# The order of ScalarE's side work in a Mamba scan: SiLUs at step 9, two normalizations at other steps

## The reference

```python
h = layernorm(layernorm(x)) * norm_w + norm_b
h = h @ in_proj_w.T                                   # 512 inner channels
h = silu(causal convolution of h, 4 taps, per channel)
dt_in, B, C = split(h @ x_proj_w.T, [1, 16, 16])
dt = softplus(dt_in @ dt_proj_w.T + dt_proj_b)
state[t] = exp(A * dt[t]) * state[t-1] + B[t] * h[t]  # 512 channels x 16 states
y[t] = sum over states (state[t] * C[t]) + D * h[t]
x1 = x + layernorm(silu(y) @ out_proj_w.T + layernorm(x))
```

## Time and profile before

| | us |
|---|---|
| median of 3 runs | 1411.33 (1410.96 to 1411.51) |
| the profiled execution, its own time | 1411.09 |
| its span in the profile | 1409.3 |
| mean granted TensorE clock | 0.941 of full speed |

### The profile page before, as it was taken

One profiled execution on the slowest core, in us unless ns is written; L12 is line 12 of the kernel. 1 busy time (PEld: TensorE's weight loads), 2 busy tenths in 40 slices (PEclk: granted clock), 3 DMA queues, 4 the chain that ended last, 5 costly groups with the idle time before them and its releaser, 6 DMA issues.

```text
span 1409.3 us, 15754 instructions
## 1 busy us (share of the span) xinstructions
PE 1175.4 (83%) x4782; PEld 518.5 (37%) x4783; DVE 1089.8 (77%) x1449; ACT 770.9 (55%) x1275; POOL 1088.4 (77%) x565
## 2 busy tenths in 40 slices
PE   5667678787886987888789688788999999999996
PEld 2222223222321422322233142233556655566653
DVE  3599999999999999999999989799241115776675
ACT  5757468676876866867686686556431111111111
POOL 0489999999999999999999999999122814444553
PEclk9898899999899999989998999999999999999998
DMA  3921211240150122014015012300269522222220
GB/s 108 274 68 62 90 60 32 75 150 0 65 192 1 62 91 106 32 75 149 1 66 175 1 62 90 134 0 31 90 238 324 162 71 82 81 81 79 83 67 15
DMA packets 72075, 127.71 MB, mean 91 GB/s; under 512 B 8759, under 2 KB 48448, under 8 KB 67904
## 3 DMA queue, kind: packets, MB, share of 16 engines
q1 hardware_dynamic: 60432, 103.72, 22.2%
q0 software_dynamic: 7152, 16.81, 3.7%
q10 hardware_dynamic: 4416, 6.29, 1.3%
HBM read 97.79 MB, written 31.76 MB: 92 GB/s over the span
## 4 chain that ended last, share of the span: by engine, by line
PE 36%; POOL 29%; issue 15%; DVE 12%; ACT 8%; DMA 0%; POOLq 0%; ACTq 0%; SPq 0%; DVEq 0%
POOL state L511 18%; PE psX L1647 10%; POOL bx L500 9%; DVE state L1090 6%; PE psX L1582 5%; PE psY L1595 3%; PE psY L1664 2%; PE bank L1664 2%; PE psY L1529 2%; PE bank L1451 2%; POOL lt L516 2%; ACT psX L763 2%; PE bank L1486 1%; DVE bx L1078 1%; DVE acc L1025 1%
## 5 line engine op out<-in xcount | busy, mean ns | idle before, releaser
L511 POOL TENSOR_TENSOR state<-state,cbc 128x1024 f32<-128x1024 f32 x256 | 606.6, 2398 | 14.9 <-DVE state L1090 14.8
L1090 DVE TENSOR_TENSOR_SCAN state<-psX,bx 128x1024 f32<-128x1024 f32 x256 | 578.5, 2279 | 38.5 <-ACT psX L763 23.1
L763 ACT ACTIVATE psX<-dt,aneg 128x511 f32<-128x511 f32 x512 | 330.7, 679 | 199.0 <-DVE state L1090 197.6
L500 POOL TENSOR_TENSOR bx<-xh,bbc 128x1024 f32<-128x1024 f32 x120 | 291.1, 2426 | 59.5 <-DMA bbc<-bc_rows 43.1
L1529 PE MATMUL psY<-state,ident 64*64 64x512 f32 x2048 | 287.5, 654 | 20.3 <-POOL state L511 20.0
L1486 PE MATMUL bank<-prow,ident 128*128 128x512 f32 x272 | 169.9, 710 | 113.3 <-DVE bx L1078 113.3
L1078 DVE TENSOR_TENSOR bx<-xh,bank 128x1024 f32<-128x1024 f32 x136 | 162.7, 1196 | 7.7 <-PE bank L1486 7.6
L1529 PEld LDWEIGHTS psY<-state,ident 64*64 64x64 f32 x2048 | 63.9, 140 | 206.8 <-issue 126.2
L961 ACT ACTIVATE sg<-psX 128x512 f32<-128x512 f32 x39 | 23.3, 597 | 196.5 <-PE psX L1647 196.5
L1486 PEld LDWEIGHTS bank<-prow,ident 128*128 128x128 f32 x272 | 48.0, 209 | 206.9 <-DVE bx L1078 166.9
L581 POOL DMA_INDIRECT ysl<-shared_rows,idx x39 | 40.3, 1033 | 80.6 <-DVE idx L1258 75.9
(11 more groups left out here) (200 smaller groups left out, 1718.8 us busy)
## 6 DMA issues: line engine op xcount, KB each, us to landing
cbc<-bc_rows SPq DMA_DIRECT2D x32, 1024.0 KB, 5.0
bbc<-bc_rows SPq DMA_DIRECT2D x16, 1024.0 KB, 6.2
slot_in<-ao SPq DMA_DIRECT2D x1, 5011.5 KB, 35.1
xsl<-slot_in SPq DMA_DIRECT2D x39, 128.5 KB, 2.0
xin<-in_x SPq DMA_DIRECT2D x8, 512.0 KB, 4.5
xr<-in_x SPq DMA_DIRECT2D x8, 512.0 KB, 5.5
x_rows<-ao SPq DMA_DIRECT2D x8, 512.0 KB, 2.9
xn_rows<-xr SPq DMA_DIRECT2D x8, 512.0 KB, 3.2
```

Of the source, the lines that this page charges most:

```text
L500: nc.gpsimd.tensor_tensor(bx[q % RB][:], xh[par][:, h * CH:(h + 1) * CH], bbc[:, n // 2].unsqueeze(1).broadcast_to([P, CH, L]), ALU.mult). ...
L511: nc.gpsimd.tensor_tensor(w[:], w[:], cbc[:, n].unsqueeze(1).broadcast_to([P, CH, L]), ALU.mult).then_inc(weighted, 1)
L763: e = nc.scalar.activation(decay[q % RD][:, c, 1:L], dt[par][:, h * CH + c, 1:L], ACT.Exp, scale=aneg[:, h * CH + c, n:n + 1])
L1090: nc.vector.tensor_tensor_scan(st[q % RS][:].rearrange("p c t -> p (c t)"), decay[q % RD].rearrange("p c t -> p (c t)"), bx[q % RB][:].rea ...
```

## The change

All three edits are on ACT's stream and in its loop over the steps. (1) The SiLU for xh, the SiLU of y and that of the shared expert, with the load of their table set before and of the other set behind, are issued at step 9 and not at step 10: after the decays for scan 11, ahead of those for scan 12. (2) The moments of `lead` (the input of batch i + 2) are computed at step 24 and not at step 29; their `apply` stays at steps 30 and 31. (3) At steps 26 and 27 `back` comes ahead of `front`: `moments(2)` and the normalizing of xn stand ahead of the second and third copy of dt. The calls behind the loop follow the new step number; the order of the work there is as before. No instruction is added or removed.

```diff
             def lead(f, par, q):
-                if q == 29:
+                if q == 24:
                     act.wait_ge(mv0_ready, f + 1)
                     moments(3, f, mv0[par], 1.0 + EPS, eps2c)
...
             def front(f, par, q):
...
-                if q == 10:
+                if q == 9:
                     act.wait_ge(conv_done, C * (f + 1))
                     if not (isinstance(f, int) and f < 2):
                         act.wait_ge(y_kept, H * (f - 1))
                     nc.scalar.activation(xh[par][:], acc[:], ACT.Silu).then_inc(xh_ready, 1)
...
             def back(b, q):
...
-                if q == 10:
+                if q == 9:
                     act.wait_ge(y_kept, H * (b + 1))
                     nc.scalar.activation(yv[:], yv[:], ACT.Silu).then_inc(ys_ready, 1)
...
             def early(q):
...
-                if q == 10:
+                if q == 9:
                     act.wait_ge(e_gate_kept, FC)
                     nc.scalar.activation(acc[:], acc[:], ACT.Silu).then_inc(e_silu, 1)
...
             def iteration(i, par, do_lead, do_front, do_scan, do_back):
...
+                    if do_back and q in (26, 27):
+                        back(i - 1, q)
                     if do_front:
                         front(i + 1, 1 - par, q)
-                    if do_back:
+                    if do_back and q not in (26, 27):
                         back(i - 1, q)
                     if not do_front:
                         early(q)
-                    if q == 10 and (do_front or do_back):
+                    if q == 9 and (do_front or do_back):
                         ln_exp_tables()
...
-            for q in range(10):
+            for q in range(9):
                 back(NB - 1, q)
             keep_y(NB - 1, 1)
-            back(NB - 1, 10)
+            back(NB - 1, 9)
```

## The result

The changed kernel takes 1413.97 us (median of 20 runs, 1412.78 to 1416.42); the kernel before, run beside it, 1411.53 us (20 runs, 1410.09 to 1414.35). The ratio is 1.0017, 95% interval 1.0011 to 1.0023: about 2.4 us slower, where the forecast was 9 us faster and the range ended at 1410.5. Of every program one execution was profiled; the changed kernel's took 1414.7 us, with a span of 1412.9.

A forecast was written before the change was run, and what follows sets the result against it. POOL's own work and a slightly longer chain over all engines bound the scan iterations, POOL's waits capping the gain. Terms of 0.65 + 1.7 + 2 x 1.15 + 2 x 2.1 = 8.85 us gave 1402.4 us, range 1398 to 1410.5.

The forecast's parts named there:

- The bound: In the scan iterations, POOL's work and a chain over all engines run almost level; POOL's waits cap the gain.
- The sum up to iteration 6: Gains of 0.65 us from iteration 0, 1.7 from 1, 1.15 per short and 2.1 per long interval: 8.85 us.
- The lead moments: Moved from step 29 to 24, they free scan 0's decays: 1.46 us won in long intervals, 1.25 in short.
- long interval: The intervals after iterations 3 and 5, with POOL waits of about 3 us; short ones follow 2 and 4.
- The swap: Moments and normalizing ahead of dt's copies, steps 26 and 27: 0.4 us won in long intervals, 0.3 lost in short.
- the sign of being wrong: Steps 26 and 27: second dt copy over 1 us late in all iterations, with PE behind it.
- The SiLUs, 0.2 us: SiLUs and table loads from step 10 to 9: chain gains 0.2 us per iteration, bounds 0 and 0.7.
- so it doesn't: Step 9, iteration 4: the table load need not wait for the convolution; scan 12 has 0.5 us in hand.
- After iteration 6 there is nothing to win: Behind iteration 6 POOL has no more waits, so no gain was counted there.
- The sentence on the tail's SiLU: The tail's SiLU moves by one step number only and keeps its place; no size given.
- Its start follows line 516 by a fixed distance, which the change leaves alone: Argument against the slower case: the start of DVE's minimum at steps 22 and 23 keeps its distance.
- The rival: Slower: DVE's minimum is held up against POOL, 5 us per event, a loss from the third on; chance 0.10.

The follow-up runs named there:

- a_again: The changed kernel unaltered, in a second set of runs: 1414.06 us, ratio 1.0015 to the kernel before.
- d_mom: The kernel before with only the lead moments moved from step 29 to 24: 1405.78 us, ratio 0.9963.
- d_swap: The kernel before with only the order at steps 26 and 27 changed: 1414.18 us, ratio 1.0016.
- a_silu7: The changed kernel with the SiLUs and table loads of iteration 7 alone back at step 10: 1410.65 us, ratio 0.9993.
- d_silu: The kernel before with only the SiLUs and their table loads moved to step 9: 1418.17 us, ratio 1.0033.
- d_mom_swap: The kernel before with the moments at step 24 and the new order at steps 26 and 27, SiLUs left at step 10: 1404.38 us, ratio 0.9951.
- a7_delay: a_silu7 plus four useless DVE statistics (1.4 us) at step 18 of iteration 6 only, delaying scan 19: 1404.47 us, ratio 0.995.

## Why the prediction was wrong, step by step

**The bound: right.** POOL against a chain over all engines, with POOL's waits at step 19 as the cap. The cap was even reached: in the last interval, from iteration 5 to 6, the changed kernel won 2.96 us, and the wait there had been 2.90.

**The sum up to iteration 6: right mechanism, a size off.** Forecast 0.65, 1.7, 1.15, 2.1, 1.15 and 2.1 us, 8.85 together. The starts of line 516 give 0.56, 0.87, 0.88, 0.56, 1.13 and 2.96: 7.0 us, and 7.9 in a_again. The 0.7 us more that came ahead of the first of them are not the change's: that start lies anywhere from 133.3 to 136.8 us in these programs, and at 136.5 in a_again. Put in one after the other, the parts give 4.3 (moments), 1.5 (order) and 1.1 us (SiLUs).

**The lead moments, "DVE waited 1.46 us": the term that was mis-sized.** It was put at 1.46 us in a long interval and 1.25 in a short one. d_mom won 0.7 and 2.0 us in the long ones (3 to 4, 5 to 6) and 0.3 and 0.5 us in the short ones (2 to 3, 4 to 5). The decay factors came early, as forecast, but the step did not ask what is late next. After iteration 3, with the decays ready at 522.79 + 1.29 = 524.1, scan 0 still waits. DVE's row, and PE's last rows of the step:

```profile
525.52 2.29 DVE L1092 TENSOR_TENSOR_SCAN state<-psX,bx 128x1024 f32<-128x1024 f32 x1 [1.20 <-issue]
```

```profile
523.62 1.02 PE L1488 MATMUL bank<-prow,ident 128*128 128x512 f32 x2
524.58 1.95 PE L1531 MATMUL psY<-state,ident 64*64 64x512 f32 x16
```

The first eight of the sixteen matmuls of line 1531 end at about 525.5, half way through the row, and PE had no pause from 507.4 on. The scan overwrites a state that PE must have read (its wait on `summed`). In d_mom the profile names it outright, with the whole of the old stall:

```profile
525.20 2.29 DVE L1090 TENSOR_TENSOR_SCAN state<-psX,bx 128x1024 f32<-128x1024 f32 x1 [1.46 <-PE psY L1529]
```

After iteration 2, where PE is not late, the wait of 1.25 us went wholly (scans 31 and 0 run as one from 406.06 on), and still that interval won only 0.3 us in d_mom: where the rest went isn't known.

**The swap: charged 0.3 us in the short intervals, gained 0.4 in the long.** d_swap gives 117.95 - 117.28 = 0.7, 0.8 and 1.0 us lost in the intervals that start at iterations 1, 2 and 4, and 0.4 and 0.9 won in those from 3 and 5. The loss was above the bound of 0.65, and the intervals became nearly level, 117.3 to 118.1 us: PE does stand behind the later copy (0.67 us idle for it in iteration 2 of d_swap). Beside the moments the order cost nothing in the short intervals (0.03 won, 0.02 lost) and won 0.9 and 0.2 us in the long ones. In the changed kernel the second dt copy of iteration 2 came where it was forecast, at 395.80, 23.42 us behind line 516, where it had been 21.53; in iteration 3 it was 0.7 us late, as forecast too. So the sign of being wrong, over 1 us late in all iterations, didn't show.

**The SiLUs, 0.2 us: the step "so it doesn't" failed in the very iteration it was worked out for.** The prediction read from the start of the kernel that the table load need not wait for the convolution. In iteration 4 it did: the block began about 1.0 us later than forecast, with 0.5 us in hand, and scan 12 waited 0.53 us. ACT's timeline:

```profile
563.54 1.28 ACT L660 ACT_TABLE_LOAD   x1 [0.98 <-DVE acc L1027]
```

It begins 0.1 us after the convolution's end, 561.14 + 2.29 = 563.43. Iteration 2 has the same wait; in iterations 0, 1, 3, 5 and 6 the load begins 0.86 us before the convolution ends, as the prediction had it, and in 1, 3 and 5 scan 12 doesn't wait. The same two iterations stand out in the profiles of a_again, a_silu7 and d_silu. Beside the two other parts (changed kernel against d_mom_swap) the SiLUs win 0.5, 0.7 and 0.7 us in the intervals that end in iterations 3, 5 and 6, and lose 0.0 and 1.0 us in those that end in 2 and 4. That fits, but nothing was run to test it, and why the load waits in these two is open.

z began 574.75 - 488.22 = 86.5 us behind line 516 and not 579.41 - 491.26 = 88.2: 1.6 us earlier where I allowed 0.2. Of this 0.6 us is an earlier broadcast on PE, as forecast the place from which xh's product follows, and the rest is the product itself, which took 3.70 us and not 4.85 (granted clock 1.00 of full speed over it, and 0.76 before). DVE's add of the output projection came only 0.6 us earlier, counted in the same way (588.03 in place of 591.65), which is the 0.56 us that this interval won. d_silu by itself won 2.5 us over the six intervals, with +1.7 and -1.5 us in single ones and 3.0 in the last.

**"After iteration 6 there is nothing to win": failed.** There was nothing to win, and something to lose. The sentence on the tail's SiLU is right, but it speaks of the calls behind the loop; iteration 7's block, inside it, got no term at all. The place at step 9 was found free in iteration 4, where DVE has its convolution (2.29 us) and statistics (1.4 us and more); iteration 6 has no statistics, and scan 12 waited 1.22 us; iteration 7 has neither, scan 12 waited 3.44 us, PE then started 128x512 matmuls after 3.22 us of idleness at a slower pace (3.65 us for four in place of 1.98; granted clock 0.66 from 928 to 933 us), and the whole cost 3.3 us (a_silu7).

**"Its start follows line 516 by a fixed distance, which the change leaves alone": failed, and it was the larger error.** The sentence is true (6.60 us before, 6.61 after) and proves nothing. What the change altered was the pause 13 us before. The rival had the mechanism right, the wrong condition and the wrong count: one event was enough, since its price was 6.2 us by a7_delay against a_silu7 and not 5, and the other loss stood beside it. The trace held the clue: the only starved minimum of the kernel before was in iteration 0, of the seven iterations with a minimum the only one without a wait at step 19.

By the measured parts: 1411.5 - 7.0 + 6.2 + 3.3 = 1414.0, and 1413.1 with a_again's 7.9, against 1413.97.

The rule that was weighed, the drain on top of a table load (ScalarE: Activation LUTs, What ACT_TABLE_LOAD costs, in the Trainium skill), did not come true here: both loads of iteration 7 took 1.28 us, with 0.02 us or less ahead of them and behind them. The rule that DVE instructions with two SBUF inputs contend with POOL (GPSIMD Engine Reference, 1. Specifications, in the Trainium skill) did, at 8.25 us against 1.35.

**What stays open:** why an unbroken run of POOL starves DVE. The shortest pause with which it did not happen was 0.42 us; what lies between that and none wasn't tried. Nor was a pause placed on purpose elsewhere than at step 19 or right at the minimum; but iteration 0 had pauses of 0.86, 0.86 and 0.36 us of POOL's, the last 32 us ahead of line 516, and its minimum starved all the same, so a pause 39 us before the minimum doesn't do and one 13 us before it does. For iteration 0 the account rests on this agreement alone: no run gave it a pause at step 19.

## What to carry to other kernels

Before a wait of the bounding engine is closed, look at what else lives on that gap: here a wait of 1 us that was put back was worth 6 us, and an explicit wait of 1.2 us, placed where the other engine needs its turn, was the fastest of all. A step that is moved because other work covers it must be checked in the first and the last iterations, where the cover may be missing. And an oddity that shows in one iteration of eight (8.26 us in place of 1.36) is to be explained before it is called a rival: ask what that iteration lacks.

## What the runs showed of the hardware that was not expected

DVE's `scalar_tensor_tensor` with two SBUF operands (128x1024, f32), issued while POOL runs a chain of f32 products, either takes 1.35 us and stretches POOL's product from 2.38 to 3.36 us, or takes 8.25 us and ends 1.1 us after POOL has run dry. In both cases it ends 1.1 us after a product of POOL's: after the one that was running when it was issued (841.32 + 2.39 = 843.71 in a7_delay, the minimum ends at 844.78), or after the last of the chain. So it works for about 1.1 us and waits for the rest, in the long case while POOL starts three more products. A pause of POOL of 0.42 to 3.3 us some 13 us earlier (18 where both halves stand at step 24) goes with the first case, none with the second, in all the programs above but the two in which POOL waits for the minimum. Two of them issued back to back beside POOL took 4.74 us, and 3.12 apart.
